# Two-layer graph attention on one core: x in chunks of 2, 2, 4 and 8 tiles, tiles 0 and 1 summed together while V is made, and VectorE's order for tiles 0 to 6 written out

## The reference, cut to what matters

```python
h = maximum(layernorm(x), 0)                # layer 0
Wh = h @ W
e = Wh @ a[:256] [:, None] + (Wh @ a[256:]) [None, :]
att = softmax(where(adj == 0, -1e9, e), axis=1)
x = x + leaky_relu(att @ Wh, 0.2)
h = maximum(layernorm(x), 0)                # layer 1
e = leaky_relu(h @ a1[:256] + (h @ a1[256:]).T, 0.01)
x = x + softmax(where(adj > 0, e, -9e15), axis=1) @ h
```

## Time and profile before

| what | value |
|---|---|
| median of 3 runs | 1689.78 us (1688.65 to 1690.71) |
| the profiled execution | 1692.08 us, span 1689.8 us |
| mean granted TensorE clock | 0.973 of full speed |
| busy: TensorE | 1551.9 us, 92% |
| busy: VectorE | 1256.5 us, 74% |
| busy: ScalarE | 989.3 us, 59% |
| layer 0, from TensorE's first projection to its last sum | 16.85 to 1061.2 us |

### The profile page before, as it was taken

How to read it: one execution, slowest core, us unless ns; L and a number is a source line. 1 busy time by engine, 2 the same in 40 slices (tenths; PEclk the granted TensorE clock), 3 DMA queues, 4 the chain that set the end, 5 groups by cost and what they waited for, 6 DMA issues and landing times. The chain is left out here.

```text
span 1689.8 us, 37172 instructions
## 1 busy us (share of the span) xinstructions
PE 1551.9 (92%) x13443; PEld 1323.6 (78%) x13443; DVE 1256.5 (74%) x4759; ACT 989.3 (59%) x1514; POOL 564.1 (33%) x588
## 2 busy tenths in 40 slices
PE   6877999999999999999999999486898999989896
PEld 5645888888888888888888888374687877877685
DVE  6577998998898899887874443696866667666765
ACT  5978656665765566566666661675645445444542
POOL 0000000000000000000014453587777777777776
PEclk9998999999999999999999999798999999999998
DMA  9418989888988898898889994555444444444443
GB/s 312 170 49 331 349 303 372 320 293 317 369 312 295 332 357 307 302 373 320 341 328 380 397 363 106 176 133 156 117 133 110 133 122 131 116 138 117 125 119 106
DMA packets 141700, 406.91 MB, mean 241 GB/s; under 512 B 25857, under 2 KB 91586, under 8 KB 108834
## 3 DMA queue, kind: packets, MB, share of 16 engines
q1 hardware_dynamic: 116114, 335.11, 54.1%
q0 software_dynamic: 25488, 70.77, 14.7%
HBM read 365.39 MB, written 40.41 MB: 240 GB/s over the span
## 5 line engine op out<-in xcount | busy, mean ns | idle before, releaser
L1016 PE MATMUL banks<-HV,adjT 128*128 128x257 f16 x8192 | 939.6, 274 | 17.1 <-DVE adjT L673 9.4
L1016 PEld LDWEIGHTS banks<-HV,adjT 128*128 128x128 fp8e4 x8192 | 792.9, 98 | 149.0 <-DVE HV L703 23.1
L1750 PE MATMUL banks<-Vp,adjp 128*128 128x257 f16 x2304 | 450.3, 277 | 80.3 <-DVE adjp L1562 64.0
L458 ACT ACTIVATE adj_f<-adj_i 128x2048 fp8e4<-128x2048 int32 x256 | 480.1, 1898 | 5.5 <-DMA adj_i<-in_adj 5.5
L1334 POOL DMA_INDIRECT gat<-h_of_layer,rec x393 | 423.0, 1076 | 121.1 <-issue 115.6
L1750 PE MATMUL banks<-Vn,adjn 128*128 128x257 f16 x2304 | 449.7, 277 | 0.0
L1750 PEld LDWEIGHTS banks<-Vp,adjp 128*128 128x128 fp8e4 x2304 | 224.5, 98 | 124.0 <-issue 61.3
L440 POOL DMA_DIRECT2D xr<-x_after_layer x46 | 25.8, 561 | 834.1 <-DVE rank L941 772.4
L1750 PEld LDWEIGHTS banks<-Vn,adjn 128*128 128x128 fp8e4 x2304 | 227.0, 99 | 36.3
L1369 ACT ACTIVATE adjn<-h1bc,nh 128x384 fp8e5<-128x384 f32 x384 | 202.4, 603 | 0.0
L1390 ACT ACTIVATE e<-gat,hb 128x4 f32<-128x4 f32 (+3 forms) x168 | 41.2, 293 | 241.9 <-DMA gat<-h_of_layer,rec 241.9
(11 more groups left out here) (172 smaller groups left out, 1481.9 us busy)
## 6 DMA issues: line engine op xcount, KB each, us to landing
adj_i<-in_adj SPq DMA_DIRECT2D x256, 1024.0 KB, 7.3
h_of_layer<-hh SPq DMA_DIRECT2D x64, 129.0 KB, 6.9
hs<-h_of_layer SPq DMA_DIRECT2D x64, 129.0 KB, 3.3
xt<-in_x SPq DMA_DIRECT2D x64, 128.0 KB, 7.0
packed_adj<-pk SPq DMA_DIRECT2D x64, 128.0 KB, 6.7
x_after_layer<-x SPq DMA_DIRECT2D x64, 128.0 KB, 7.1
HV<-in_x SPq DMA_DIRECT2D x14, 512.0 KB, 8.8
gat<-h_of_layer,rec POOLq DMA_INDIRECT x393
```

The costliest lines, as they stand in the source:

```text
L458: nc.scalar.activation(adj_f[:, b, q * QC:(q + 1) * QC], adj_i[:, q, :], ACT.Copy, scale=2.0, saturate=False).then_inc(conv_done, 1)
L1016: last = nc.tensor.matmul(acc[b][:, 0:DV], adjT_h[:, b, i, q, :, h], V0[:, jb, s, 0:DV], start=(jb == 0 and s == 0), stop=(jb == T - 1 and ...
L1750: mm = nc.tensor.matmul(bank[2 * i + part][:, 0:DV], m[:, i * P:(i + 1) * P], V[:, j, s, 0:DV], start=(j == 0 and s == 0), stop=(j == T - ...
```

## The change

x comes in chunks of 2, 2, 4 and then 8 tiles, and the first three go through statistics, roots and ReLU one after the other. TAKE is 18. There are ten converts in the projection stage, after tiles 20, 24, ... 56. For the tile before each of these VectorE copies the transposes (`take_hT`), in place of ScalarE. Tiles 0 and 1 of rows are summed together, four matmuls for each tile of V. The fold, words and masks of tile 2 are made while V is made, and its masks and sums have their own places. VectorE's order up to step 6 is written out, and the `turn` of tiles 3 to 6 sits later in the tile before. The loops over V are unrolled. The diff, cut to its core (the helpers `place_of_words`, `sums_of`, `close_sums` and `close_dots` only choose buffers or bundle calls; the written order ends with `decode(0, 1)`, `close_dots(3)`, `whole_fold(7)`, `close_sums(4)`, `scale_h(4)`, `extract(5, 1)`, `make_keys(6, 0)`, `decode(0, 2)`, `close_dots(4)`, `extract(6, 2)`, `decode(0, 3)`, `make_keys(7, 1)`):

```diff
     XC = 8
-    EDGES = [0, 2] + list(range(XC, N // P + 1, XC))
+    EDGES = [0, 2, XC // 2] + list(range(XC, N // P + 1, XC))
     NCH = len(EDGES) - 1
-    TAKE = 24
+    DIRECT = 3
+    TAKE = 18
...
+            adjT2 = sb("adjT2", [P, HALF, BQ * P], u16)
-            fold1 = sb("fold1", [P, 2, 2, GW], i32)
+            fold1 = sb("fold1", [P, 4, 2, GW], i32)
...
-            CONVERTS = list(range(T - 2 * Q * 4 - 4, T - 4, 4))
-            FOLDS = {CONVERTS[Q - 1] + 3: 0, CONVERTS[2 * Q - 1] + 3: 1}
+            CONVERTS = list(range(T - 2 * Q * 4 - 12, T - 4, 4))
+            FOLDS = {T - TAKE + 1: 0, CONVERTS[2 * Q - 1] + 3: 1}
+            BY_DVE = [t - 1 for t in CONVERTS]
+            THIRD = bank[4]
...
                 def copy_hT(t):
+                    if t in BY_DVE:
+                        return
...
-                            convert(k // Q, k // Q, [k % Q], True)
+                            convert(k // Q, k // Q % 2, [k % Q], k < 2 * Q)
...
-                roots(0)
-                relus(0)
-                roots(1)
-                for c in range(2, NCH):
+                for c in range(DIRECT):
+                    roots(c)
+                    relus(c)
+                for c in range(DIRECT, NCH):
                     roots(c)
...
-                    relus(c - 1)
+                    if c > DIRECT:
+                        relus(c - 1)
...
                 for t in range(2):
                     copy_words(t, t, t, None)
+                convert(2, 0, range(len(CONVERTS) - 2 * Q, Q), False)
...
-                for t in range(SH):
-                    weigh(t, True)
-                for t in range(SH, VU):
-                    weigh(t, False)
-                with act.Fori(1, T // VU) as k:
-                    for j in range(VU):
-                        weigh(k * VU + j, False)
+                for t in range(T):
+                    weigh(t, t < SH)
+                    if t == VU + SH - 1:
+                        convert(3, 1, range(0, 1), False)
+                    if t == 2 * VU - 1:
+                        copy_words(2, 0, 2, None)
+                    if t == 3 * VU + SH - 1:
+                        convert(3, 1, range(1, 2), False)
...
-                convert(2, 0, range(0, Q), False)
-                convert(3, 1, range(0, Q // 2), False)
-                copy_words(2, 0, 2, None)
                 convert(3, 1, range(Q // 2, Q), False)
+                copy_sums(0, 0)
+                convert(4, 0, range(0, 1), False)
+                copy_sums(1, 1)
+                convert(4, 0, range(1, 2), False)
+                roots1(0)
+                copy_words(3, 1, 3, None)
+                convert(4, 0, range(2, 3), False)
                 act.wait_ge(hh_ones, 1)
-                for t in range(1, 2 * NX):
-                    step(t, t % NX, 16 if t > NX else None, 16 * ((t + 1) // NPK) or None, words=t > 1)
+                finish(0, 0)
+                convert(4, 0, range(3, 4), False)
+                for t in range(2, 2 * NX):
+                    step(t, t % NX, 16 if t > NX else None, 16 * ((t + 1) // NPK) or None, words=t > 4,
+                         sums=t > 2, next_words=t < 4)
...
+                def take_hT(t):
+                    dve.wait_ge(tr_ready, t + 1)
+                    dve.wait_ge(proj_ready, t - 1)
+                    nc.vector.tensor_copy(hT[:, t % 2, :, :].rearrange("p c n -> p (c n)"), tps[t % 2][:, 0:D])\
+                        .then_inc(hT_taken, 1)
+
                 def take_wh(t):
+                    if t + 1 in BY_DVE:
+                        take_hT(t + 1)
                     dve.wait_ge(proj_ready, t + 1)
...
-                statistics(1)
-                scales(1)
+                for c in range(1, DIRECT):
+                    statistics(c)
+                    scales(c)
                 dve.wait_ge(ones_set, 2)
-                for c in range(2, NCH):
+                for c in range(DIRECT, NCH):
                     statistics(c)
-                    if c > 2:
+                    if c > DIRECT:
                         scales(c - 1)
...
-                with dve.Fori(0, T // VU) as k:
-                    for j in range(VU):
-                        t = k * VU + j
+                for t in range(T):
...
+                    if t == VU - 1:
+                        for part in range(4):
+                            fold(2, 0, part)
+                    if t == 3 * VU - 1:
+                        unpack(2, 0, 2)
...
-                for t in range(2):
-                    make_keys(t, t)
-                    extract(t, t)
-                for part in range(4):
-                    fold(2, 0, part)
+                make_keys(0, 0)
+                extract(0, 0)
+                normalise(0, 0)
+                normalise(1, 1)
+                make_keys(1, 1)
+                whole_fold(3)
+                close_sums(0)
+                extract(1, 1)
+                scale_h(0)
+                unpack(3, 1, 3)
                 make_keys(2, 0)
                 dve.wait_ge(hh_ones, 1)
-                for t in range(1, T):
+                close_dots(0)
+                close_sums(1)
+                whole_fold(4)
+                extract(2, 2)
+                scale_h(1)
+                make_keys(3, 1)
+                close_dots(1)
+                unpack(4, 0, 0)
+                normalise(2, 0)
+                whole_fold(5)
+                close_sums(2)
+                scale_h(2)
+                extract(3, 3)
+                normalise(3, 1)
+                unpack(5, 1, 1)
+                decode(0, 0)
+                make_keys(4, 0)
+                close_dots(2)
+                whole_fold(6)
+                close_sums(3)
+                scale_h(3)
+                extract(4, 0)
+                make_keys(5, 1)
+                normalise(4, 0)
+                unpack(6, 0, 2)
...
+                for t in range(6, T):
...
                 pe.wait_ge(w_in, 16 * 3)
-                pe.wait_ge(ucol_ready, 2)
...
+                def first_two(turn_at):
+
+                    pe.wait_ge(adjT_ready, 2)
+                    pe.sem_inc(masks_due, 1)
+                    for jb in range(T):
+                        pe.wait_ge(v0_ready, jb + 1)
+                        q, i, h = place(jb)
+                        for b in range(2):
+                            for s in range(2):
+                                last = nc.tensor.matmul(acc[b][:, 0:DV], adjT_h[:, b, i, q, :, h],
+                                                        V0[:, jb, s, 0:DV], start=(jb == 0 and s == 0),
+                                                        stop=(jb == T - 1 and s == 1))
+                            if jb == T - 1:
+                                last.then_inc(acc_ready, 1)
+                        if jb == turn_at:
+                            turn(2, 0)
...
-                aggregate(0, 0, v0_wait=True, reuse=False, turn_at=None)
-                aggregate(1, 1, reuse=False, turn_at=3 * T // 4)
-                with pe.Fori(1, SORT // 2) as k:
+                first_two(3 * T // 8)
+                aggregate(2, 0, 5 * T // 8)
+                aggregate(3, 1, 7 * T // 16)
+                aggregate(4, 0, T // 4)
+                aggregate(5, 1, 3 * T // 8)
+                with pe.Fori(3, SORT // 2) as k:
```

More of the change, by code:

```diff
@@ L316, in two_layer_graph_attention, with place_of_words, sums_of, copies_before @@
             SPARSE, DENSE = SP0, -NS
-            CONVERTS = list(range(T - 2 * Q * 4 - 4, T - 4, 4))
-            FOLDS = {CONVERTS[Q - 1] + 3: 0, CONVERTS[2 * Q - 1] + 3: 1}
+            CONVERTS = list(range(T - 2 * Q * 4 - 12, T - 4, 4))
+            FOLDS = {T - TAKE + 1: 0, CONVERTS[2 * Q - 1] + 3: 1}
+            BY_DVE = [t - 1 for t in CONVERTS]
+            THIRD = bank[4]
+            def place_of_words(t, b):
+                return t if isinstance(t, int) and t in (2, 3) else b
+            def sums_of(t, b):
+                return THIRD if isinstance(t, int) and t == 2 else acc[b]
+            def copies_before(t):
+                return sum(1 for u in range(t + 1) if u not in BY_DVE)
             def offset(t):
@@ L546, in copy_sums, with step @@
                         act.wait_ge(lr_ready, t)
-                    nc.scalar.activation(ysb[:, :], acc[b][:, 0:D], ACT.Copy, scale=rden[:, b:b + 1])\
+                    nc.scalar.activation(ysb[:, :], sums_of(t, b)[:, 0:D], ACT.Copy, scale=rden[:, b:b + 1])\
                         .then_inc(ysb_ready, 1)
-                def step(t, j, reuse, pk_reuse, converts=True, words=True):
+                def step(t, j, reuse, pk_reuse, converts=True, words=True, sums=True, next_words=False):
                     if converts:
@@ L555, in step @@
                         copy_words(t + 1, (j + 1) % 2, (j + 1) % NPK, pk_reuse)
-                    copy_sums(t - 1, (j - 1) % 2)
+                    if sums:
+                        copy_sums(t - 1, (j - 1) % 2)
                     if converts:
```

(48 more changed lines are left out.)

28 lines of the change are left out of this document (19 added, 9 removed).

## The result

The changed kernel takes 1703.03 us (median of 4 runs, 1701.17 to 1706.07) where the kernel before took 1689.39 in the same comparison: 0.79% longer, ratio 1.0079 with a 95% interval of 1.0064 to 1.0094. I had forecast slower, but by 4.9 us, not 13.6, and the time lies outside my range. The profiled execution took 1706.07 us, its span is 1704.3.

The account below looks back on a forecast made before the run. TensorE, 92% busy, was taken as the bound, with VectorE almost the bound from V to tile 8. V 9.4 us later less 4.5 won there made 4.9 us slower: 1694.7 us, range 1686.5 to 1701.

Parts of the forecast that it names:

- Part 1, the early start: Start to projection 3: fewer tiles' statistics come ahead of it, so projection 3 starts 6.0 us earlier, at 16.9.
- Part 2, the holes: Projections: with TAKE = 18 TensorE idles 2.3 us at six chunk borders; with table load and last fold 17.8 us lost.
- Part 3, conversions: Projection stage: ten conversions in place of eight cost 7.5 us, where the eight took about 10.
- The clock, and a rule: TensorE's clock: it fell some 4 us into one stall; new holes of 2.3 us are shorter, so no loss counted there.
- As a rival I had this at 0.03: Projections: the clock falls at every hole, seven times 2.7 us, adding 19 us: 1713.6 us; chance 0.03.
- The rival of a slow clock at the start or at tile 8: Start or tile 8: one more slow stretch like the first three projections' 2.7 us gives 1697.4 us; chance 0.12.
- Part 4, V to tile 8: From V to tile 8: VectorE wins 11.2 us of its idle time less 6.5 of new waits, 4.5 us won.
- The rival that no holes open: Projections: the 17.8 us of holes are gone, V starts 8.4 us earlier, time 1676.9 us; chance 0.10.

Follow-up runs that it names:

- The filled kernel: The changed kernel with TensorE transposes of the identity, which add nothing to the result, put in the holes (the one before projection 54 left empty): 1697.93 us.
- two edits: Each on the changed kernel with TAKE = 20: ScalarE's copy of tile 6's words one step earlier, 1678.93 us; VectorE's masks of tiles 7 and 8 first, 1680.03 us.
- the chunks alone: The kernel before with only the chunks of 2, 2, 4 and 8, TAKE = 18 and the order these need; eight conversions, no joint sum: 1704.49 us.

## Why the prediction was right and wrong

- **Part 1, the early start: right within 0.9 us, and partly by luck.** Projection 3 at 17.81, not 16.9. Projection 0 came at 9.71, 1.6 us earlier than I had it, and at my pitches projection 3 would have followed at 15.7. Instead TensorE idled 1.97 us for the take. VectorE had waited 1.27 us for the 8-tile chunk of x to land, which I had not priced. So the take set the start, and not TensorE's pace.
- **Part 2, the holes: right.** The chain measured 3.36 us, and the holes stand where I put them. The seven, with their slower restarts, add up to 17.9 us for my 17.8, and 19 and 20 for TAKE show the room that I had worked out.
- **Part 3, conversions: right, about 1 us too dear.** Without its slow projections the changed kernel needs 90.0 us from projection 3 to 63, where my sum had 91.0. The filled kernel says the same. It needs 92.3, of which 1.5 are slow projections behind projection 3 and 0.9 those behind the hole at 54: from there to 56 it took 3.96 us, against 3.05 in the changed kernel.
- **"The clock, and a rule": the step that failed.** I took 4 us, the time after which the clock had fallen in one stall, for the least idle that does it, and so put the clock's loss in the projections at nothing. Behind idles of 2.1 us it was low at projections 6, 14 and 22, behind 3.46 us at 46, and behind the wait of 1.97 us at projection 3; it wasn't at 30, 38 and 54. Against the same projections at the full clock that cost 1.7, 1.7, 0.9, 2.1 and 1.6 us, 8.0 in all. From projection 3 to 63 the changed kernel took 98.0 us for my 91.0, so this one step holds all of the 7.0, and the conversions gave 1.0 back. With the holes filled it was 92.3. As a rival I had this at 0.03, and priced it at seven times 2.7 us. The rival of a slow clock at the start or at tile 8 (0.12) came true at both, with 1.6 and 1.1 us. The Trainium skill's page "TensorE: Matmul & The Clock Gate", in "A second HAM failure mode: psum-queue depth-cycling", warned of frequent short idles that make the clock go up and down. Here the trace agrees with the page (half the clock in the windows of 40 to 42, 54 to 56 and 92 to 94), and my reading of the earlier trace rows, that idles of 0.85 us hadn't done it, said nothing about idles of 2.1.
- **Part 4, V to tile 8: right in kind, 2 us too good.** The three new waits of VectorE that I found are there: 1.18 us for the dots of tile 1, 0.97 for the masks of tile 5 and 2.76 for those of tile 6, for my 1.4, 1.1 and 3.0. Tile 8 won 3.5 us instead of 4.5; then 1.1 were lost again up to layer 1, which the slow matmuls at the start of tile 8 account for (2.31 us for 1.28), and 2.4 were left. That VectorE's queue is the bound is shown by two edits: a wait of 2.75 us taken from it moved everything behind by as much, and another order of the same work moved nothing. I had left the slow clock at tile 8 out of the sum, since I looked only at tile 7.

Together: 0.9 at the start, 7.0 in the projections and 2.1 after V, less 0.5 between the last projection and V, is 9.5: the 14.4 that was measured in place of 4.9.

The rival that no holes open was false for TAKE = 18 and described TAKE = 20: my price for it was 12.9 us faster than the kernel before, and 7.2 was measured (1680.56 for 1687.78). The start of V was priced at 97.2 (8.4 us earlier) and came at 101.20, in part by the wait for the adjacency and by slow projections behind projection 3 (18.34 to 22.27 for two, where 2.18 us are the rule).

## What to carry to other kernels

Where one engine both takes results away and prepares the next inputs, count how many results of room lie between the last take and the first input that depends on what follows it, and compare them with the length of the chain; here one unit of a constant moved V by 15 us (18 to 19), and the next by 6 (19 to 20). A hole in TensorE's work costs more than its length if the clock falls behind it, so price each at both clocks. On an engine whose queue is nearly full, moving an instruction only moved the wait here, and taking away what the engine itself waited for brought all of it.

## What was not expected of the hardware

Idles of 2.1 us of TensorE, each in the same pattern of work, were followed by half the clock in some places and by the full one in others (40 to 42 and 54 to 56 against 66 to 68 and 78 to 80 in the changed kernel). Which ones fall isn't a matter of the place: behind the same hole of 2.1 us before projection 14, the projections are slow in the changed kernel and fast in the chunks alone, and before 30 it is the other way round. What decides it, these runs don't show. Idles of 1.0 us (TAKE = 19) were followed by it nowhere, and where transposes of the identity filled the same 2.1 us, the clock stayed full. The early chunks of x, once the holes are gone, bring almost nothing: V starts at 101.20 with them (TAKE = 20) and at 101.41 without. Projection 3 starts 4.3 us earlier with them, and at projection 20 only 0.7 us of it is left (40.83 for 41.54), since the first conversion waits for its quarter of the adjacency.

The granted clock doesn't show every slow matmul: in the kernel before, projections 0 to 2 follow each other every 2.0 us, as at the low clock, and the windows from 18 to 22 us still say 1.00. What slowed them isn't shown.
